# Row tiles of 100 partitions fetched as 64 and 36 partitions, per batch, in place of 96 and 4

## The reference

```python
x = x + tanh(g_xattn[0]) * perceiver_attention(ctx_1024, layernorm(x), mask, ...)   # "a"
x = x + tanh(g_ffn[0])   * top2_of_4_experts(layernorm(x), ...)                      # "f"
x = x + tanh(g_xattn[1]) * strided_attention(layernorm(x), ctx_1024, ...)            # "g"
x = x + tanh(g_ffn[1])   * top2_of_8_experts(layernorm(x), ...)                      # "m"
```

## Time and profile before

| | us |
|---|---|
| median of 3 runs (lowest, highest) | 2138.17 (2137.04, 2138.41) |
| the profiled execution, its own time | 2129.79 |
| its span, first to last instruction | 2128.1 |

### The profile page before, as it was taken

How to read it: one execution, slowest core, us unless ns; L and a number is a source line. 1 busy time by engine, 2 the same in 40 slices (tenths; PEclk the granted TensorE clock), 3 DMA queues, 4 the chain that set the end, 5 groups by cost and what they waited for, 6 DMA issues and landing times. The chain is left out here.

```text
span 2128.1 us, 35623 instructions
## 1 busy us (share of the span) xinstructions
PE 1928.1 (91%) x12328; PEld 1568.5 (74%) x12328; DVE 1017.5 (48%) x2242; ACT 844.0 (40%) x1791; POOL 664.7 (31%) x555
## 2 busy tenths in 40 slices
PE   5799999999999999999769999999985885999983
PEld 3478878787777778787558888888873675999982
DVE  6324555555555555544464333333334457554544
ACT  3233444334444344344344343333312434655540
POOL 4021110303030301100045544555521104787862
PEclk9999999999999999999979999999997897999996
DMA  8620101010101101000053332233339116545546
GB/s 219 220 93 1 58 9 52 19 52 19 52 11 37 34 16 55 9 17 17 13 183 109 115 118 71 87 109 109 114 135 301 43 59 198 171 166 176 180 144 199
DMA packets 111816, 201.58 MB, mean 95 GB/s; under 512 B 31424, under 2 KB 32224, under 8 KB 111156
## 3 DMA queue, kind: packets, MB, share of 16 engines
q1 hardware_dynamic: 106052, 178.88, 26.7%
q0 software_dynamic: 4800, 15.73, 2.2%
q10 hardware_dynamic: 816, 5.05, 0.6%
HBM read 171.64 MB, written 27.98 MB: 94 GB/s over the span
## 5 line engine op out<-in xcount | busy, mean ns | idle before, releaser
L462 POOL TENSOR_TENSOR a_rows<-a_rows,a_gain_x 128x512 f32<-128x512 f32 (+1 forms) x48 | 71.2, 1484 | 551.4 <-DVE a_rows L877 551.4
L621 PE MATMUL a_kv_ps<-a_kvin_hi,a_wk_hi 128*128 128x512 f32 (+1 forms) x512 | 196.2, 383 | 1.0 <-DVE a_kvin_lo L884 1.0
L1095 PE MATMUL f_banks<-f_wab_hi,f_x_hi 128*128 x448 | 185.0, 413 | 0.8 <-DVE f_h_sb L1773 0.5
L622 PE MATMUL a_kv_ps<-a_kvin_lo,a_wk_hi 128*128 128x512 f32 (+1 forms) x512 | 180.4, 352 | 0.0
L623 PE MATMUL a_kv_ps<-a_kvin_hi,a_wk_lo 128*128 128x512 f32 (+1 forms) x512 | 180.3, 352 | 0.0
L1097 PE MATMUL f_banks<-f_wab_hi,f_x_lo 128*128 x448 | 176.9, 395 | 0.0
L1096 PE MATMUL f_banks<-f_wab_lo,f_x_hi 128*128 x448 | 175.4, 392 | 0.0
L544 ACT ACTIVATE a_probs<-a_probs,a_neg_max 100x822 f32<-100x822 f32 x128 | 125.9, 984 | 113.1 <-DVE a_neg_max L908 112.9
L1773 DVE TENSOR_TENSOR f_h_sb<-f_h_sb,f_banks 128x256 f32<-128x256 f32 x112 | 47.2, 421 | 242.0 <-ACT f_h_sb L1494 241.0
L1494 ACT ACTIVATE f_h_sb<-f_banks 128x256 f32<-128x256 f32 x112 | 43.0, 384 | 290.9 <-PE f_banks L1097 290.9
L621 PE MATMUL a_kv_ps<-a_wv_hi,a_kvin_hi 128*128 128x512 f32 (+1 forms) x384 | 156.6, 408 | 1.0 <-DVE a_k_lo L901 1.0
(11 more groups left out here) (401 smaller groups left out, 4870.3 us busy)
## 6 DMA issues: line engine op xcount, KB each, us to landing
f_raw<-f_pieces SPq DMA_DIRECT2D x94, 256.0 KB, 2.7
m_raw<-m_pieces SPq DMA_DIRECT2D x92, 256.0 KB, 3.0
f_wab_raw<-f_pieces SPq DMA_DIRECT2D x42, 512.0 KB, 6.5
m_wab_raw<-m_pieces SPq DMA_DIRECT2D x42, 512.0 KB, 6.4
a_rows<-ctx SPq DMA_DIRECT2D x8, 1280.0 KB
ahead_piece<-g_ctx SPq DMA_DIRECT2D x3, 2880.0 KB, 25.9
a_wout_sb<-L_xattn_Wkv SPq DMA_DIRECT2D x8, 512.0 KB, 11.6
m_y_acc<-m_pieces SPq DMA_DIRECT2D x8, 512.0 KB, 7.6
```

The source lines that it names most:

```text
L462: own.link(nc.gpsimd.tensor_tensor(row, row, gain_x[0:n, :], ALU.mult))
L621: nc.tensor.matmul(out, hi_l, hi_r, start=first, stop=False)
L622: nc.tensor.matmul(out, hi_l, lo_r, start=False, stop=False)
L1095: nc.tensor.matmul(out, left_hi, right_hi, start=start, stop=False)
```

## The change

Partitions 0 to 63 and 64 to 99 replace 0 to 95 and 96 to 99 everywhere, and no load gathers the remaining partitions of several batches for y any more. At the start of stage a the number of DMAs stays (four). A half of the sums is fetched as two DMAs for x of four batches and two per batch for y: ten in place of eight. At the end of stage m, 16 loads replace nine; DVE waits for both parts of its batch instead of for the rest of all batches. The stores of even batches become 64 and 36 partitions.

```diff
@@ stage a
-                for p in (slice(0, EVEN), slice(EVEN, M)):
+                for p in PARTS:
@@
-EVEN = 96
+PARTS = (slice(0, 64), slice(64, 100))
@@ gated_experts, SP
             if x_out is None:
-                for n in range(handed.RING // 2):
-                    handed.load_pair(sp, n)
-                    if n == 0:
-                        handed.load_rest(sp, 0)
+                handed.load_half(sp, 0)
                 return
@@
-            sp.dma_start(of_tokens(y_got[EVEN:M, :, :, :]), rows[EVEN:M, :, :]).then_inc(y_rest, 16)
             for b in range(B):
-                sp.dma_start(of_tokens(y_got[0:EVEN, b:b + 1, :, :]), rows[0:EVEN, b:b + 1, :]).then_inc(y_loaded[b], 16)
+                for p in PARTS:
+                    sp.dma_start(of_tokens(y_got[p, b:b + 1, :, :]), rows[p, b:b + 1, :]).then_inc(y_loaded[b], 16)
@@
-                for at, first, end in ((0, 0, EVEN), (EVEN, EVEN, M)) if b % 2 == 0 else ((TURN, 0, M - TURN), (0, M - TURN, M)):
+                for at, first, end in ((0, 0, M - TURN), (M - TURN, M - TURN, M)) if b % 2 == 0 else ((TURN, 0, M - TURN), (0, M - TURN, M)):
@@ gated_experts, DVE
             dve.wait_ge(x_again, 16)
-            dve.wait_ge(y_rest, 16)
             for b in range(B):
-                dve.wait_ge(y_loaded[b], 16)
+                dve.wait_ge(y_loaded[b], 32)
@@ SumsAhead (load_rest and load_pair are gone)
+    def load_half(self, eng, h):
+        M, half = self.M, range(self.RING * h, self.RING * h + self.RING)
+        for p in PARTS:
+            eng.dma_start(self.x_mid[p, half.start:half.stop, :], self.x_in[half.start:half.stop, p, :].rearrange("b p d -> p b d")).then_inc(self.x_loaded[h], 16)
+        for b in half:
+            rows = self.y_pairs[1 + TOP * M * b:1 + TOP * M * (b + 1), :].rearrange("(m k) d -> m (k d)", k=TOP)
+            for p in PARTS:
+                eng.dma_start(self.of(b).rearrange("p k d -> p (k d)")[p, :], rows[p, :]).then_inc(self.y_loaded[b], 16)
@@ strided_attention, SP
-            for n in range(RING // 2, B // 2):
-                sums.load_pair(sp, n)
-                if n == RING // 2:
-                    sums.load_rest(sp, 1)
+            sums.load_half(sp, 1)
@@ strided_attention, DVE, combine(b)
-                if b % 2 == 0:
-                    dve.wait_ge(x_loaded[b // 2], 16)
-                dve.wait_ge(y_loaded[b], 16)
                 if b % RING == 0:
-                    dve.wait_ge(sums.rest_loaded[b // RING], 32)
+                    dve.wait_ge(x_loaded[b // RING], 32)
+                dve.wait_ge(y_loaded[b], 32)
```

More of the change, by code:

```diff
@@ L1240, in gated_experts @@
         y_loaded = [sem(f"y_loaded{b}") for b in range(B)]
-        y_rest = sem("y_rest")
         x_again = sem("x_again")
@@ L1879, in __init__ @@
         self.y_more = ctx.enter_context(nc.sbuf_tensor("sums_y_more", [P, B - self.RING, TOP, D], F32))
-        self.x_loaded = [nc.alloc_semaphore(f"sums_x_loaded{n}") for n in range(B // 2)]
+        self.x_loaded = [nc.alloc_semaphore(f"sums_x_loaded{h}") for h in range(2)]
         self.y_loaded = [nc.alloc_semaphore(f"sums_y_loaded{b}") for b in range(B)]
-        self.rest_loaded = [nc.alloc_semaphore(f"sums_rest_loaded{h}") for h in range(2)]
     def of(self, b):
         return self.y_got[0:self.M, b, :, :] if b < self.RING else self.y_more[0:self.M, b - self.RING, :, :]
[L1887 to L1901, removed]
+    def load_half(self, eng, h):
[6 more added lines that the diff above has]
+                eng.dma_start(self.of(b).rearrange("p k d -> p (k d)")[p, :], rows[p, :]).then_inc(self.y_loaded[b], 16)
 def strided_attention(nc, x_in, y_pairs, gates, ahead, sums, wq_t, bias_qkv, wo_t, bo, gate, x_out, routing):
```

## The result

The changed kernel takes 2141.09 us (median of 11 runs, 2138.05 to 2145.98), the kernel before beside it on the same chip 2137.04 (median of 11, 2132.77 to 2139.13). The ratio is 1.0022, interval 1.0012 to 1.0032: 4.7 us slower by the ratio (the medians differ by 4.1), where 5.9 us faster had been forecast. The profiled execution took 2143.93 us, 1.7 more than its span of 2142.2. It is 14.1 longer than the profiled one of before. Intervals vary too.

What follows compares the result with a forecast made beforehand. PE was taken to bound the kernel, at 91% busy, with only its waits for touched loads able to move. Start -1.0, seam -2.6 and end -2.3 sum to -5.9 us: 2138.2 becomes 2132.3, range 2126 to 2143.

Steps and rivals of the forecast that it cites:

- What bounds the kernel: Whole kernel: PE is busy 91%; only stretches where PE stands for a touched load, at start, seam and end, can move.
- The rest loads make the slumps: Seam and end: loads of partitions 96 to 99 of several batches cause three stretches at 102 to 106 GB/s, costing 6 us.
- P = 1.9: All touched loads: DMA time in us for y of one batch, 100 rows of 4 KB, 0.41 MB; bounds 1.66 to 2.5.
- the low one: Lower bound of P, 1.66: all rows move at the 247 GB/s of 96-partition loads, without slumps.
- The high rival: Every batch: partitions 64 to 99 slump, P = 2.5, +8.4 us, 2146.6; chance of slower 0.20.
- Start, -1.0: Stage a: the a_lat loads, 4P, end earlier and DVE and PE follow; -1.0 us, bounds -2.0 to +1.4.
- Seam, -2.6: Between stages f and g: each half of the sums 1.3 less, so piece 2 reaches PE 2.6 us earlier; bounds -5.5 to +4.6.
- The wait that had been looked for as late next: Seam: DVE's start, forecast at 1609.2 against 1612.25, and ACT's bias load, gaining 1.3, were both judged early enough.
- End, -2.3: Stage m: DVE starts five us earlier but waits for each batch, ending 2.3 us earlier; bounds 4.3 gained to 2.4 lost.
- its own sign: End of stage m: the prediction is wrong if the spacing of batches is above 2.1 us.
- The sum: Whole kernel: -1.0 - 2.6 - 2.3 = -5.9 us, giving 2132.3 us.

Runs made afterwards that it cites:

- the separate parts: End of stage m of the kernel before, y loaded as partitions 0 to 63, 64 to 95, 96 to 99, each for all batches; 2145.6 us, single execution.
- the kernel whose pieces wait for half 0: Kernel before with only the sums' loads at 64 and 36, plus SP waiting for half 0's last y before weights and piece 1; 1.0011, 2137.6 us.
- the seam alone: Kernel before with only the sums' loads between stages f and g made as 64 and 36 partitions in the change's order; 1.0019, 2151.0 us.

## Why the prediction was wrong, point by point

*What bounds the kernel.* Right. The three stretches are where the times moved, and at the seam PE's last wait is still the one for piece 2.

*The rest loads make the slumps.* Right, and now shown: in every kernel without them at a place the slump is gone there, they move at 33 GB/s alone, and with them cut up per batch the kernel is 8 to 9 us faster. The reckoned cost of the slumps (6 us at seam and end) is near the 7.1 that this version gains in the profile.

*P = 1.9.* About right while all engines work, and too low for a half as a whole. Half 0 went at 215 GB/s (1.91), the end at 1.94 and 2.13 in two kernels, the separate parts at 2.0. But in the kernel whose pieces wait for half 0, SP goes on at 1616.62, 14.6 behind its first load: half 0 took just as long as before (1616.2 - 1601.56), less the lead 12.7 or 2.1 per P, as four engines are through early. The bound that failed is the low one: 96 rows at 247 is no price for 64 and 36. What the Trainium skill gave (2.1, SBUF — State Buffer, "Door 1") was nearer to the end of the changed kernel than the choice of 1.9. The high rival (2.5, a slump in every batch) is refuted: the first batch of the end took 2.4, but the average is 2.13.

*Start, -1.0.* The sign was wrong in the profile: 0.5 to 1.5 later, 0.2 to 1.1 with this part alone; the timing of that part doesn't tell it from zero. The step that failed is the one that let part of an unexplained 2.8 us go. And "DMAs and bytes are the same" put the issue at nothing, while the four take SP 1.06 us longer and the first packet starts 0.5 later in both kernels.

*Seam, -2.6.* This is the failed step, and it is the whole loss: +5.3 in the profile, +4.3 with the seam alone (4.3 and 3.3 against the mean of 45.7), timed at 1.0019, 4.1 us. The working took a half of the sums, weights and pieces as loads that follow each other, each at its own rate. The 1.3 us per half that it counted as gained were not there: half 0 as a whole took what it took before (P above), and DVE's start came 1.4 earlier relative to SP's first load, not three. And a term was missing, the handover from a load of 36 rows to a large one and on to the next half. For the time from 1630 to 1640 the DMA view of the changed kernel gives 1.80 MB. Of it, 0.96 MB are piece 1's (166 packets of 5760 bytes in the trace): 2.3 us at 412; the other 0.84 MB at 215 is 3.9. So 3.8 of these 10 us are contention by this estimate, and 26.4 against 30.25 with 32 in place of 36 says 3.8 too. With the 2.6 that were not gained (at most, as four engines go on to the next loads meanwhile), the estimate is -2.6 + 2.6 + 3.8 = +3.8, between the 3.3 and 4.3 of the two kernels. "The DMA engines have a backlog then, so nothing starves" was true, and just this backlog did the harm: it let half 1 in beside piece 1. The wait that had been looked for as late next (DVE's start, ACT's bias) wasn't; PE's wait for piece 1, which before had no idle time in front of it, hadn't been looked at.

Smaller: the first work of PE in stage g came 7.5 us behind SP's first load, not 5.9 (5.0 + 0.91). The ten issues of half 0 take 1.28 + 4.35 in place of eight with some 0.4 each, and PE's idle time of 8.25 covers it, as had been said.

*End, -2.3.* Right in kind, under half in size. DVE starts 4.4 behind the first y load (3.8 forecast), but with 2.13 per batch in place of 1.9 it is done 0.6 earlier than before; with this part alone 1.94 and 1.7. Against the mean of the seven old ends (20.8) that is 0.4 and 1.5. By its own sign, a spacing above 2.1, the prediction was wrong in the change and not with this part alone. The time can't tell either from zero.

*The sum.* The three parts timed alone make -0.0007 + 0.0019 - 0.0002 = 0.0010, the change itself 0.0022, each with an interval of about 0.0012 to either side; no interplay is needed to join them. In the profiles, against the means of the old code, start, seam and end are +1.0, +4.3 and -0.4, 4.9 together, against 4.7 timed. Of the rivals none had this: the slower one put the loss into each batch, while it lies in the handover between loads. That the time lies inside the stated range is luck: the range reached that far for a slump in every batch, which did not happen.

*A version that beats both* follows from the part that was right: 96 and 4 per batch, 0.9958 and 0.9954 of before in two sessions, some 14 us less than the change.

## What to carry to other kernels

Where a tile doesn't fill the even count of partitions, put the small remainder load directly behind the large one of its own batch; don't gather the remainders of several batches in one load, and don't recut the large one for its sake. Reckon a queue not as a sum of loads at their own rates only: look at what stands behind a load that splits unevenly, because a following large load can end slowly, beside the next one, and whoever waits for it waits longer. And in the profile ask of each wait whether it has idle time in front of it; the one with none is the next to become late.

## What the runs showed of the hardware

- 64 and 32 partitions moved at the same 208 and 207 GB/s, 96 at 247, 128 at 412 to 421; four alone at 33. Behind four-partition loads over four or eight batches the whole core moved 102 to 106, though loads of 96 were queued with them.
- Loads of 64 and 36 rows leave the 16 DMA engines out of step: at the end of such a half, and of the large load behind it, 12 packets were in flight (78% of the queue's share in place of 102 to 107). Loads of 100 rows had 10 in flight (64.7%).
- After loads of 36 rows, with more such loads behind, the tail of a 128-partition load ran at 144 to 153 GB/s for four to six microseconds with all DMA engines busy, its packets nearly three times as long (0.65 us in place of 0.22). After 32 rows, or with either neighbour held back, it did not.
- A load of 100 partitions in one went at 2.4 us per batch of 0.41 MB at first and settled at 1.8.
- Four loads of 64 and 36 rows took SP 2.69 us to issue, four of 96 and 4 rows 1.63.
- Two holes that waits on SP opened in the DMA stream, each about 3 us long, cost nearly as much as the contention that they avoided.
